# Cross-attention and a gated mixture on one core: the loads of k, x, the values and the residual begun by ScalarE instead of by the sync queue

## The reference

```
x   = x + gamma * attention(layernorm(x), ctx, ctx)      # 4 batches x 8 heads
x   = x + mixture(layernorm(x))

attention: q, k, v are cut along the SEQUENCE axis into 8 heads of 128 rows each
  qk = einsum('bhdq,bhdl->bhql', q, k) / sqrt(128)       # 1024 queries x 1024 keys, 128 deep
  p  = softmax(qk)
  o  = einsum('bhql,bhdl->bhdq', p, v)                   # back to 128 rows x 1024
mixture (8 experts of rank 64):
  h = relu(x @ W1 + b1);  alpha = softmax(h @ W2 + b2)
  out = sum_k alpha_k * U_k (V_k x)
```

## Time and profile before

| what | us |
|---|---|
| runs (3): lowest, median, highest | 1683.01, 1687.66, 1691.62 |
| the profiled execution, its own time | 1685.4 |
| its span in the trace | 1683.6 |
| PE busy | 1568.5 (93%) |
| DVE busy | 993.7 (59%) |
| ACT busy | 765.0 (45%) |
| POOL busy | 715.3 (42%) |

### The profile page before, as it was taken

The page is one execution under the profiler, slowest core; times in us unless marked ns, Lnnn a source line. Parts: engine busy times, 40 slices in busy tenths (PEclk is TensorE's granted clock), DMA queues, the critical chain, the costliest instruction groups (busy, mean ns, idle before and its releaser), DMA issues.

```text
span 1683.6 us, 21711 instructions
## 1 busy us (share of the span) xinstructions
PE 1568.5 (93%) x6496; PEld 1159.5 (69%) x6496; DVE 993.7 (59%) x1290; ACT 765.0 (45%) x1222; POOL 715.3 (42%) x523
## 2 busy tenths in 40 slices
PE   5989999898999989999967999999999999999999
PEld 3666666666666666666645787877878787787877
DVE  7888888888888888888754432433323242332312
ACT  5776766767676676767653312112121211212120
POOL 3887878888788887878751000000000000000000
PEclk9999999999999999999987999999999999999999
DMA  6989989999899888998886031120302112030302
GB/s 176 283 270 287 264 285 273 275 286 267 285 262 290 281 268 284 264 294 277 240 265 220 20 101 50 63 87 6 130 13 100 50 62 87 10 133 6 100 1 75
DMA packets 119963, 294.18 MB, mean 175 GB/s; under 512 B 26240, under 2 KB 31360, under 8 KB 119936
## 3 DMA queue, kind: packets, MB, share of 16 engines
q1 hardware_dynamic: 119936, 293.84, 56.3%
HBM read 125.87 MB, written 33.69 MB: 95 GB/s over the span
## 4 chain that ended last, share of the span: by engine, by line
PE 49%; POOL 26%; issue 15%; DMA 4%; SPq 3%; DVE 2%; ACT 1%; POOLq 0%; ACTq 0%; DVEq 0%
PE scores L928 21%; POOL pt_lo L342 15%; PE scores L971 11%; PE attended L989 10%; POOL k_lo L325 4%; POOL x_out L351 3%; PE spare L1008 2%; DMA x_res<-in_x 2%; SPq L223 2%; POOL v_lo L329 2%; PE scores L517 1%; PE scores L946 1%; PE scores L943 1%; DMA pt<-pb 1%; PE attended L539 1%
## 5 line engine op out<-in xcount | busy, mean ns | idle before, releaser
L342 POOL TENSOR_TENSOR pt_lo<-pt,pt_hi 128x512 fp32r<-128x512 f32 (+1 forms) x256 | 399.7, 1562 | 156.5 <-ACT pt_hi L411 156.5
L571 DVE TENSOR_REDUCE neg_max<-scores 128x1 f32<-128x1024 f32 x256 | 312.6, 1221 | 105.8 <-PE scores L517 105.5
L418 ACT ACTIVATE probs<-scores,neg_max 128x1024 f32<-128x1024 f32 x256 | 284.2, 1110 | 198.8 <-DVE neg_max L571 198.5
L580 DVE STREAM_TRANSPOSE pb<-probs 128x1024 f32<-128x1024 f32 x256 | 316.2, 1235 | 16.8 <-DMA pt<-pb 16.5
L853 POOL TENSOR_TENSOR rstd<-var_eps,minus_half 128x1 f32<-128x1 f32 x28 | 17.2, 613 | 609.6 <-DVE var_eps L1054 609.6
L517 PE MATMUL scores<-k_hi,q_hi 128*128 128x512 f32 x512 | 237.1, 544 | 20.5 <-ACT probs L418 11.3
L539 PE MATMUL attended<-pt_hi,v_hi 128*128 128x512 f32 x320 | 140.9, 440 | 88.4 <-POOL pt_lo L342 87.6
L411 ACT ACTIVATE pt_hi<-pt 128x512 fp32r<-128x512 f32 (+1 forms) x256 | 186.7, 729 | 63.8 <-DMA pt<-pb 59.2
L872 ACT ACTIVATE hidden<-scores,b_col 128x512 f32<-128x512 f32 x64 | 44.2, 690 | 351.3 <-PE scores L928 351.3
L928 PE MATMUL scores<-nt_hi,w_hi 128*128 128x512 f32 x512 | 200.9, 392 | 2.5 <-DVE w_lo L1079 2.5
L928 PE MATMUL scores<-nt_lo,w_hi 128*128 128x512 f32 x512 | 200.2, 391 | 0.0
(11 more groups left out here) (95 smaller groups left out, 2640.9 us busy)
## 6 DMA issues: line engine op xcount, KB each, us to landing
pt<-pb SPq DMA_DIRECT2D x512, 256.0 KB, 4.6
x_raw<-in_x SPq DMA_DIRECT2D x32, 512.0 KB, 6.3
k_raw<-in_ctx SPq DMA_DIRECT2D x32, 512.0 KB, 5.2
gain_row<-gains SPq DMA_DIRECT2D x64, 256.0 KB, 4.8
x_res<-in_x SPq DMA_DIRECT2D x32, 512.0 KB, 5.6
x<-x_out SPq DMA_DIRECT2D x64, 256.0 KB, 4.1
first_n<-x SPq DMA_DIRECT2D x32, 512.0 KB, 3.6
result<-x SPq DMA_DIRECT2D x64, 256.0 KB, 3.7
```

Source lines behind the costliest of these rows:

```text
L342: nc.gpsimd.tensor_tensor(pt_lo[2 * parity + half][:, :, keys, :], pt[2 * parity + half][:, :, keys, :], as_f32(hi[half][q][:]), ALU.subtr ...
L418: nc.scalar.activation(probs[j % 2][:], scores[j % 2][:], ACT.Exp, bias=neg_max[:, j:j + 1], accum_out=row_sum[b][:, j:j + 1]).then_inc(s_ ...
L571: nc.vector.tensor_reduce(neg_max[:, j:j + 1], scores[j % 2][:], AX_X, ALU.max, negate=True).then_inc(s_max, 1)
L580: nc.vector.transpose(pb[half][:, :, j % HALF, :], probs[j % 2][:]).then_inc(s_blocks, 1)
```

## The change

Nothing is computed differently and no tile moves. The five loads of a slot (native values, k, x, values, residual) leave SP's queue and are written into ACT's `slot`: native values in block 2, k in block 3, x in block 4, values and then the residual in block 5, each behind that block's exponentials and high parts, and in block 3 ahead of the queries. They keep their sizes, tiles and semaphores. The residual's load gets a wait of its own for `s_added` (POOL's half-1 addition in block 3). On SP the gathers, gains and stores remain in their old order. The first loads of the prologue stay on SP, and so does the residual's load of the last head.

```diff
@@ sync: slot @@
             if last:
                 load_first(n)
-            if more:
-                sp.wait_ge(s_klo, h + 2)
-                load_k(h + 2)
             if not (known and h < 2):
                 sp.wait_ge(s_pv, n - JB)
-            load_v_native(h, parity)
-            if not last:
-                sp.wait_ge(s_vlo, h + 1)
-                load_v(h + 1)
             if not first:
                 spread_gain(h - 1, 0)
...
                 store_x1(h - 2, 1)
-            if not first:
-                load_residual(h - 1)
-            if more:
-                sp.wait_ge(s_q32, h + 2)
-                load_x(h + 2)
             gather(h, n, 0, parity)
@@ scalar: slot @@
                 if j == 2:
                     high_values(h, n, parity)
+                    if not first:
+                        load_v_native(h, parity)
+                if j == 3 and more:
+                    act.wait_ge(s_klo, h + 2)
+                    load_k(h + 2)
+                if j == 4 and more:
+                    act.wait_ge(s_q32, h + 2)
+                    load_x(h + 2)
+                if j == 5 and not last:
+                    act.wait_ge(s_vlo, h + 1)
+                    load_v(h + 1)
+                if j == 5 and not first:
+                    if not (known and h < 2):
+                        act.wait_ge(s_added, h * 2 - 2)
+                    load_residual(h - 1)
                 if j == 3 and not last:
                     queries(h + 1, 1 - parity)
```

More of the change, by code:

```diff
@@ L292, in sync @@
         load_k(1)
+        load_v_native(0, 0)
         h, n = over_heads(sp, slot)
@@ L401, in scalar, with rows_of @@
     def scalar(act):
+        def rows_of(h):
+            return bass.ts(h, P)
         def high_probs(quarter):
@@ L412, in high_probs, with load_x, load_k, load_v @@
                                  ACT.Copy).then_inc(s_pthi, 1)
+        def load_x(h):
+            act.dma_start(x_raw[:], x[rows_of(h), :]).then_inc(s_x_in, 16)
+        def load_k(h):
+            act.dma_start(k_raw[:], ctx[rows_of(h), :]).then_inc(s_k_in, 16)
+        def load_v(h):
+            act.dma_start(v_raw[:, 0:SPLIT, :], ctx_t[rows_of(h), 0:SPLIT * P].rearrange("p (b d) -> p b d", d=P)
+                         ).then_inc(s_v_in, 16)
+        def load_v_native(h, parity):
+            act.dma_start(v_nat[parity][:], ctx_t[rows_of(h), SPLIT * P:].rearrange("p (b d) -> p b d", d=P)
+                         ).then_inc(s_vn_in, 16)
+        def load_residual(h):
+            act.dma_start(x_res[:], x[rows_of(h), :]).then_inc(s_res_in, 16)
         def exps(s, j, b):
@@ L462, in slot @@
         def slot(h, n, parity, first, last):
+            known = isinstance(h, int)
+            more = not (known and h + 2 >= heads)
             for j in range(JB):
```

## The result

| | before | after |
|---|---|---|
| median of 13 runs (lowest, highest), us | 1684.38 (1680.56, 1691.62) | 1674.68 (1669.27, 1680.96) |
| ratio after / before | | 0.9938, 95% interval 0.9923 to 0.9953 |
| span of the profiled execution, us | 1683.6 | 1672.9 |

The change makes the kernel 0.6% faster. The prediction said 1.5% slower, so it had the sign wrong.

What follows compares the result with a forecast made beforehand. PE bounds the attention, with 2.3 us a head to win; the residual's ring grows to 27.4 us, 0.9 above the head's 26.5. Over 30 steps about +26 us on 1685.4, about 1711 us; range 1668 to 1750, forecast's own 1695 to 1730.

Steps and rivals of the forecast that it cites:

- ring B: Attention, once a head: residual's load, POOL's addition and double quarter, PE; 24.90 us before, 27.4 forecast after, becoming the bound.
- ring A: Attention, once a head: SP's gather of half 0, which ACT and then POOL and PE await; sets the pace before.
- Together 3.0 us in place of 0.49: Delay from block 5's exponentials to the residual's issue on ACT: quarter's end 1.73, pitch 0.46, SP's gather issues 0.8 us.
- the optimistic bound at 1.6: Lower bound in us for the residual's issue delay on ACT, if the issues run beside block 5's second quarter.
- The 0.8 us taken for issues that fall into SP's gather issues: Charge for the values' and residual's issues on ACT meeting SP's eight gather issues; range 0 to 1.9 us.
- ACT's own cost, 0.5 us: Uncovered cost on ACT of issuing k in block 3 and x in block 4; range 0 to 2.8 us.
- The flight, 6.2 us: Residual's load from issue to landing after the change; before, median 5.6 us, upper end 8.9.
- PE can win 0.5 us a head of it: PE's gain from the earlier gather of half 0, once SP no longer issues the residual and x before it.
- The upper bound of 2.3 us, from the backlog: Most the gather of half 0's ring could shorten, with the loads' 1 MB gone from its queue; at least 0.96 us.
- The 221 GB/s called SP's pace: DMA rate in the gather of half 1 with no load ahead, taken as the pace at which SP issues.
- The faster rival: Residual's ring stays at 24.9 us, under the head's 26.5; PE gets its 0.5 us: −15 us, 1670; chance 24%.
- The held-up ACT: Rival: k and x issues each cost ACT 1.4 us uncovered; about +2 us a head, 60 us, 1745; chance 12%.

Runs made afterwards that it cites:

- e6: Changed kernel with the residual's load one block later on ACT, in block 6 instead of block 5: 1738.14 us, ratio 1.0328 to the kernel before.
- e8: Changed kernel with one more wait: ACT issues block 5's values and residual loads only after its own quarter is done: 1732.86 us, ratio 1.0307 to before.
- e1: Changed kernel with k and both value loads back on SP, so only x and the residual moved: 1672.15 us, ratio 0.9924 to before.
- e2: Changed kernel with x and the residual back on SP ahead of the gather, so only k and the values moved: 1689.91 us, ratio 1.0046 to before.
- e3: Changed kernel plus two tiny 2 KB loads on SP where the residual and x stood: 1680.96 us, ratio 0.9977 to before.
- e5: Changed kernel with the loads of x and k each cut in two, seven ACT issues a slot instead of five: 1678.81 us, ratio 0.9966 to before.
- e4: Changed kernel with the residual's load one block earlier, in block 4, and x's in block 5: 1673.4 us, ratio 0.9929 to before.

## Why the prediction was wrong

*The bound and the two rings: right.* PE's wait for POOL is what moved (54.6 to 43.7 us in 24 heads). Both rings exist: e6 and e8 lengthen ring B, by 3.2 and 2.0 us to the issue, and the head grows by 2.2 and 2.1; e1, e2 and e3 act on ring A.

*The step that failed: the residual's issue, "Together 3.0 us in place of 0.49".* Measured: 0.45 us in the mean (13.36 − 12.91), 0.76 in the slot shown. Before, the mean was 0.70 (13.35 − 12.65; the 0.49 was one slot), so the residual's issue did not become later at all. I let ACT's sequencer reach the load only after the activation ahead of it had ended, and set the optimistic bound at 1.6, with the issue beside that activation. It was below even this, since the load leaves before the activation starts, in some heads before block 5's exponentials have started (by up to 0.24 us). With 3.0, ring B came to 27.4 us; with 0.45 in its place and everything else as forecast it is 24.9, under the head. e8 puts the assumed order back by one wait, with the issue at 2.40, and gives 28.1 us a head and +58 us over the changed kernel, of which the lower granted clock can account for about 6. That shows the step and, but for those 6, its price. The 0.8 us taken for issues that fall into SP's gather issues was a fair size where they do fall there: in e8 the residual's issue takes a median of 0.80 us on ACT, in the changed kernel 0.34.

The Trainium skill (Perfetto Trace Analysis, DVE / Act Engine Instruction) says that an activation is pushed into a wait queue and the sequencer is then ready for the next instruction. The rows of the changed kernel agree: x's load 1.12 us ahead of an activation that precedes it in the program. How far ahead of the activations a load can leave, the rows alone tell: the values' load went out 0.17 us behind the start of block 5's exponentials in the slot shown and 0.14 us ahead of it in the mean, the residual's 0.59 us behind the values'.

*The term of ACT's own cost, 0.5 us, was too large.* From PE's first quarter to the exponentials of block 5 it is 11.10 us against 10.96, so 0.14, and in e5, with two more issues, it is 11.10 again.

*The flight, 6.2 us, was too short.* The median rose from 5.6 to 7.0, beyond the value taken and inside the bounds (to 8.9). Alone this is worth 0.8 us and moves ring B to about 25.7; with ACT's 0.14 in place of 0.5 it is 25.3, under the 25.98 measured. This error had the opposite sign to the other two: without it the forecast would have been further off. POOL's waits of 0.7 us a head show how near it is, and e4 that it does not decide.

*Ring A, "PE can win 0.5 us a head of it": right.* The gather starts 14.32 − 13.60 = 0.7 us earlier, PE's wait falls by 0.45 and the head by 0.54. The upper bound of 2.3 us, from the backlog, did not come: the stretch behind the gather's start is 11.8 us against 11.7, and even in e3 it is shorter by only 0.6. The 221 GB/s called SP's pace was one microsecond; over the 7.24 us of that gather's issues the profile has 260. The faster rival had this mechanism and the figure, −15 us. The window gained 13.0 us, the whole execution 10.7. The keys' high part of the window's first head already stands 0.9 us later than before; the other 1.4 us is lost behind the window. The chance of 24% for this rival was too low. One unmeasured term, whose bounds were drawn too narrowly, carried the whole sign. Of that rival's own terms, the flight of 5.6 and the issue of 1.6 were both off, in opposite directions, so its figure of 24.9 us for ring B is in part luck.

*The held-up ACT* does not occur: the stretch that it would lengthen grew by 0.14 us.

## What to carry to other kernels

Where a DMA stands in ScalarE's program said little here about when it went out: x's load left 1.68 us in the mean before the activation ahead of it started, while in e8, with an explicit wait for the activation, the loads left behind it. Nor did the issues take activation time that could be seen. Check what an issue really waits for before charging it to a stage. Issue time on the sync queue is a cost when it stands just ahead of the transfer that closes a ring: two issues of 0.35 us with their pitch were about two thirds of 0.6% here, and moving the other three gained nothing. Before reordering a queue, look for a pair in it where the second waits for the first to land, and keep something long between them.

## What the runs showed of the hardware that was not expected

A DMA in ScalarE's program was issued before an activation that precedes it there had started, by 1.12 us in the slot shown and 1.68 in the mean. Its issue takes 0.34 us on the sequencer, beside running activations; in e8, among SP's gather issues, the same issue takes a median of 0.80 us.

The residual's load takes longer to land when the gather of 2 MB is beside it. With the issue 0.2 us ahead of the gather's start (the changed kernel) the median is 7.0 us; in e4, on the same second queue but 2.8 us ahead, it is 5.5, against 5.6 in one queue before; in e8, 1.6 us behind that start, it is 7.4. The gather took from start to use 11.8 us against 11.7 before, and 11.1 in e3, where the residual's load was 1.4 us ahead of it. So neither landed sooner in the changed kernel for having a second queue.
